# A cross-attention and expert layer on one core: row maxima turned in diagonal blocks, column-tile value products, the residual added in PSUM, routing in groups, a new step order

## What is computed

```python
B, S, D, H, FF, E, K = 16, 128, 128, 16, 512, 8, 2           # context rows SE = 77, HD = D // H = 8

def _attn(q_in, k_in, v_in, wq, bq, wk, bk, wv, bv, wo, bo, causal):
    Q, Kp, V = (heads of q_in @ wq + bq, k_in @ wk + bk, v_in @ wv + bv)
    scores = jnp.einsum('bqhd,bkhd->bhqk', Q, Kp) / jnp.sqrt(HD)      # causal: upper triangle -inf
    a = jax.nn.softmax(scores, axis=-1)
    return einsum('bhqk,bkhd->bqhd', a, V).reshape(B, S, D) @ wo + bo

def _moe(x, rw, rb, w1, b1, w2, b2):
    router_weights = jax.nn.softmax(x @ rw + rb, axis=-1)
    topw, topi = jax.lax.top_k(router_weights, K)
    topw = jax.nn.softmax(topw, axis=-1)
    combine = zeros((T, E)).at[rows, topi].add(topw)
    h = gelu(x @ w1[e] + b1[e]); eo = h @ w2[e] + b2[e]               # for every expert e
    return sum over e of eo * combine[:, e]

x = layernorm1(x + attn(x, x, x, sa weights, causal=True))
x = layernorm2(x + attn(x, context, context, ca weights, causal=False))
x = layernorm3(x + moe(x))
```

## Time and profile before

| | us |
|---|---|
| median of 3 runs | 497.91 (495.34 to 503.47) |
| the profiled execution: its own time | 495.67 |
| its span on the core | 493.6 |
| PE busy | 371.7 (75%) |
| DVE busy | 315.4 (64%) |
| ACT busy | 282.0 (57%) |
| POOL busy | 171.4 (35%) |

### The profile page before, as it was taken

How to read it: one execution, slowest core, us unless ns; L and a number is a source line. 1 busy time by engine, 2 the same in 40 slices (tenths; PEclk the granted TensorE clock), 3 DMA queues, 4 the chain that set the end, 5 groups by cost and what they waited for, 6 DMA issues and landing times.

```text
span 493.6 us, 8885 instructions
## 1 busy us (share of the span) xinstructions
PE 371.7 (75%) x2121; PEld 248.6 (50%) x2121; DVE 315.4 (64%) x1061; ACT 282.0 (57%) x648; POOL 171.4 (35%) x217
## 2 busy tenths in 40 slices
PE   2358779989988989999889997767603999999300
PEld 1323455565465465465465453353303999999300
DVE  9732555778778778778777877554371555555292
ACT  2017259679679679679679679516311555555132
POOL 9403112131441441431431432502120455554343
PEclk9999889999999999999999999965955999999855
DMA  8230302521341341350340340040872122221142
GB/s 223 82 74 0 71 16 49 140 51 29 84 131 30 82 134 28 82 141 19 88 131 24 88 138 12 24 137 18 259 184 52 42 70 64 60 62 51 55 124 85
DMA packets 38602, 39.92 MB, mean 81 GB/s; under 512 B 4762, under 2 KB 32271, under 8 KB 38552
## 3 DMA queue, kind: packets, MB, share of 16 engines
q1 hardware_dynamic: 36280, 35.11, 27.1%
q0 software_dynamic: 2272, 4.24, 2.5%
HBM read 13.66 MB, written 14.79 MB: 58 GB/s over the span
## 4 chain that ended last, share of the span: by engine, by line
PE 31%; DVE 25%; issue 11%; ACT 7%; DVEq 7%; DMA 7%; SPq 5%; POOL 3%; POOLq 0%; ACTq 0%
PE bank L535 6%; PE bank L479 4%; PE bank L522 4%; SPq L366 4%; DVEq L980 4%; PE bank L480 3%; DMA sa_km<-sa_ku 3%; ACT sa_qm L674 3%; PE bank L503 3%; DVE ca_nm L810 3%; DVE ca_us L983 2%; PE bank L502 2%; DVE yb L993 2%; PE bank L546 2%; ACT ca_qm L674 2%
## 5 line engine op out<-in xcount | busy, mean ns | idle before, releaser
L733 ACT ACTIVATE sa_us<-bank,expert_b 128x128 f32<-128x128 f32 x156 | 44.9, 367 | 48.8 <-PE bank L617 39.9
L1051 POOL TENSOR_SCALAR_AFFINE_SELECT sa_pt<-sa_pt 128x512 f32<-128x512 f32 x64 | 39.0, 635 | 71.5 <-ACT sa_pt L682 71.3
L1083 POOL DMA_INDIRECT results<-sa_us,xs x39 | 41.0, 1052 | 51.9 <-DVE sa_us L995 44.8
L810 DVE TENSOR_REDUCE sa_nm<-bank 128x4 f32<-128x512 f32 x64 | 41.6, 684 | 16.7 <-PE bank L503 16.5
L1074 POOL DMA_INDIRECT dispatched<-r_sent,r_row x32 | 31.8, 994 | 44.0 <-DVE r_sent L936 36.6
L617 PE MATMUL bank<-xsT,ca_us 128*128 128x128 f32 x312 | 45.2, 290 | 2.2 <-DVE ca_us L983 1.6
L674 ACT CAST sa_qm<-bank 8x512 fp32r<-8x512 f32 x64 | 36.9, 576 | 14.0 <-PE bank L510 12.4
L628 PE MATMUL bank<-ca_pt,sa_us 128*128 x312 | 43.8, 284 | 0.1
L674 ACT CAST ca_qm<-bank 8x512 fp32r<-8x512 f32 x64 | 36.8, 575 | 10.4 <-PE bank L510 9.2
L617 PEld LDWEIGHTS bank<-xsT,ca_us 128*128 128x128 f32 x312 | 39.4, 198 | 4.9 <-issue 3.1
L682 ACT ACTIVATE sa_pt<-bank 128x512 f32<-128x512 f32 x64 | 34.8, 597 | 10.4 <-PE bank L522 10.4
(11 more groups left out here) (210 smaller groups left out, 851.9 us busy)
## 6 DMA issues: line engine op xcount, KB each, us to landing
dispatched<-filler SPq DMA_DIRECT2D x17, 520.0 KB, 4.4
sa_km<-sa_ku SPq DMA_DIRECT2D x32, 96.0 KB
sa_qm<-sa_qu SPq DMA_DIRECT2D x32, 96.0 KB
ca_qm<-ca_qu SPq DMA_DIRECT2D x32, 96.0 KB
xs<-dispatched SPq DMA_DIRECT2D x39, 65.0 KB
sa_pt<-in_e_w SPq DMA_DIRECT2D x8, 256.0 KB, 5.2
ca_pt<-in_e_w SPq DMA_DIRECT2D x8, 256.0 KB, 6.1
sa_pt<-results SPq DMA_DIRECT2D x8, 256.0 KB, 4.7
```

The lines of the kernel that those rows point to most:

```text
L733: act.activation(hid[b][:, c, :], bank[2 * b + c // 2][:, P * (c % 2):P * (c % 2) + P], ACT.Gelu, bias=b1[:, bass.ds(expert * FC + c, 1)]) ...
L810: dve.tensor_reduce(k.nm[:, u, g, :], bank[home[k, "scores", u][g % 2]][:, :].rearrange("q (j n) -> q j n", j=J)[:, :, 0:k.keys], AX.X, AL ...
L1051: pool.affine_select(out=blockg, in_=blockg, compare_op=ALU.is_ge, fill=0.0, base=0, pattern=[[0, J], [1, P]], channel_multiplier=-1).then ...
L1083: pool.indirect_dma_start(out=results, out_offset=bass.IndirectOffsetOnAxis(ap=xs[v][:, P:P + 1].bitcast(I32), axis=0), in_=ys[v], in_offs ...
```

## The change

- `shift`: `mm` becomes [128, 2, 4, 4, 32], of which only the diagonal blocks are written; four transposes instead of one give `mT` with each head's maximum on its own 32 rows and columns, and ACT copies it once (128 x 512) in place of four casts. `weights` adds it by a second matmul for each group, with the selector `pick` (the rows `kones` broadcast) as stationary operand. The first matmul no longer waits for `shift`.
- `spread_terms`: the copies by SP take all 32 rows of each block (were 24), and DVE's operation is a plain copy.
- `mix`: 16 stationary operands of 32 columns for a sequence; each head goes to a column tile of its own, moving operand 128 columns, so one bank holds the whole sequence; one ACT copy and one `restore` of 4 transposes for a sequence where there were two.
- `norm`: one step for a pair. PE adds the residual into the bank by a matmul with the identity, for CA the bias by another; DVE no longer adds, and writes straight to `residual`, which `turn` and `route` read; POOL only takes the power, once for both.
- Routing in groups of pairs (0, 1), (2, 3, 4), (5, 6), (7): the logits of each pair are collected, and 27 DVE operations run once for the group on up to 6 tiles; the rank matmuls use totals of earlier groups; the indirect DMAs of a group (8, 12, 8, 4) go out together.
- `xs`, `ys`, `hid` and some table rows lie in tiles that the attention has done with. `ORDER` and `home` are new.

The core of the diff:

```diff
+def routed_together(pairs):
+    groups, left = [], list(range(pairs))
+    for size in (2, 3, 2):
+        if len(left) > size:
+            groups.append(tuple(left[:size]))
+            left = left[size:]
+    return groups + [(p,) for p in left]
...
         ORDER = [
+            (CA, 'restore', 1, -2), (CA, 'turn', 0, -1), (CA, 'mix', 2, -2), (CA, 'mix', 3, -2), (SA, 'shift', 0, 0),
+            (CA, 'project', 0, -1), (SA, 'values', 0, 0), (SA, 'turn', 0, 1), (CA, 'restore', 3, -2),
+            (CA, 'turn_heads', 0, -2), (CA, 'spread_terms', 0, -1), (RT, 'fill', 0, -2), (CA, 'spread_terms', 1, -1),
+            (CA, 'turn_heads', 1, -2), (CA, 'norm', 0, -2), (SA, 'weights', 0, 0), (SA, 'scores', 2, 0),
+            (RT, 'route', 0, -2), (RT, 'gate', 0, -2), (SA, 'scores', 3, 0), (SA, 'weights', 1, 0),
+            (SA, 'mix', 0, 0), (SA, 'shift', 1, 0), (RT, 'choose', 0, -2), (CA, 'scores', 0, -1),
+            (SA, 'weights', 2, 0), (RT, 'second', 0, -2), (CA, 'scores', 1, -1), (SA, 'mix', 1, 0),
+            (SA, 'weights', 3, 0), (RT, 'place', 0, -2), (CA, 'shift', 0, -1), (RT, 'number', 0, -2),
+            (CA, 'scores', 2, -1), (SA, 'project', 0, 1), (SA, 'restore', 1, 0), (SA, 'mix', 2, 0),
+            (SA, 'spread_terms', 0, 1), (SA, 'spread_terms', 1, 1), (SA, 'mix', 3, 0), (CA, 'weights', 0, -1),
+            (CA, 'scores', 3, -1), (CA, 'values', 0, -1), (SA, 'restore', 3, 0), (SA, 'turn_heads', 0, 0),
+            (CA, 'weights', 1, -1), (SA, 'turn_heads', 1, 0), (CA, 'shift', 1, -1), (CA, 'mix', 0, -1),
+            (CA, 'mix', 1, -1), (CA, 'weights', 2, -1), (SA, 'scores', 0, 1), (SA, 'norm', 0, 0),
+            (SA, 'scores', 1, 1), (CA, 'weights', 3, -1)]
...
                 for j in range(J):
-                    rows = slice(32 * j + 8, 32 * j + 32)
+                    rows = slice(32 * j, 32 * j + 32)
...
             def shift(k, p, u):                                      # TensorE
-                pe.transpose(bank[home[k, "shift", u][0]][:, 0:P], k.mm[:, u].rearrange("q j r -> q (j r)").bitcast(F32), ident).then_inc(k.s_mt_ps, 1)
+                for j in range(J):
+                    ins = pe.transpose(bank[home[k, "shift", u][0]][:, P * j:P * j + P], k.mm[:, u, j].rearrange("q i r -> q (i r)").bitcast(F32), ident)
...
             def weights(k, p, part):
-                pe.wait_ge(k.s_sha, p * 8 + 4 * u + 4)
...
+                    pe.matmul(bank[b][0:k.keys, :], k.ku[:, g, k.keys * u:k.keys * u + k.keys], k.qm[:, :, g, P * u:P * u + P], start=True, stop=False)
+                pe.wait_ge(k.s_sha, p * 2 + u + 1)
+                for g in pair:
+                    b = home[k, "weights", u][g % 2]
+                    pe.matmul(bank[b][0:k.keys, :], pick[:, g, 0:k.keys], k.mT[:, u].rearrange("r j n -> r (j n)"), start=False, stop=True).then_inc(k.s_s2_ps, 1)
...
             def mix(k, p, part):
-                    ins = pe.matmul(bank[b][64 * (g % 2):64 * (g % 2) + 64, :], k.vo[:, u, g, :], k.pt[u][:, 512 * g:512 * g + 512], start=True, stop=True)
+                    for j in range(J):
+                        ins = pe.matmul(bank[b][32 * j:32 * j + 32, P * g:P * g + P], k.vo[:, u, J * g + j, :],
+                                        k.pt[u][:, 512 * g + P * j:512 * g + P * j + P], start=True, stop=True)
...
             def norm(k, p, u):
+                pe.matmul(both, ident, residual[:, 2 * p:2 * p + 2, :], start=True, stop=False)
+                if not k.causal:
+                    pe.matmul(both, ident, k.bo.rearrange("q (o d) -> q o d", o=1).to_broadcast([P, 2, D]), start=False, stop=False)
+                for v in range(2):
+                    pe.wait_ge(k.s_ot, p * 2 + v + 1)
+                    ins = pe.matmul(both[:, v], k.oT[:, v, :], k.wo[:, :], start=False, stop=(v == 1))
...
             def shift(k, p, u):                                      # ScalarE
-                for j in range(J):
-                    rows = slice(32 * j, 32 * j + 8)
-                    src = bank[home[k, "shift", u][0]][rows, 0:P].rearrange("r (o n) -> r o n", o=1).to_broadcast([8, GROUPS, P])
-                    act.copy(k.qm[rows, j, :, P * u:P * u + P], src).then_inc(k.s_sha, 1)
+                act.copy(k.mT[:, u].rearrange("r j n -> r (j n)"), bank[home[k, "shift", u][0]][:, :]).then_inc(k.s_sha, 1)
...
             for k in KINDS:                                          # VectorE, setup
-                setup(dve.memset(k.vo[:, :, :, 32:64], 1.0))
-                setup(dve.memset(k.mm[:, :, :, :].bitcast(F32), 0.0))
+                setup(dve.memset(k.vo[:, :, :, HD:HD + 1], 1.0))
+                setup(dve.memset(k.vo[:, :, :, HD + 1:], 0.0))
+                setup(dve.memset(k.mm[:, :, :, :, :].bitcast(F32), 0.0))
...
+            setup(dve.tensor_copy(pick[:, :, :], kones.rearrange("r (g o) -> r g o", o=1).to_broadcast([P, GROUPS, P])))
...
             def number(k, p, u):                                     # GpSimd
+                n, group = group_of[p]
+                if p != group[-1]:
+                    return
                 pool.wait_ge(s_filled, p * 32 + 32)
...
-                for v in range(2):
+                for v in range(2 * len(group)):
                     for c in range(TOPK):
                         pool.indirect_dma_start(out=dispatched, out_offset=bass.IndirectOffsetOnAxis(ap=r.row[:, v, c:c + 1], axis=0),
```

More of the change, by code:

```diff
@@ L278, in build @@
-            (CA, "weights", 1, -1), (SA, "norm", 1, 0), (CA, "weights", 2, -1), (RT, "number", 0, -2),
-            (CA, "restore", 0, -1), (CA, "mix", 1, -1), (SA, "scores", 0, 1), (CA, "weights", 3, -1),
-            (CA, "restore", 1, -1), (CA, "mix", 2, -1), (SA, "scores", 1, 1), (CA, "turn_heads", 0, -1),
-            (CA, "turn", 0, 0), (RT, "fill", 0, -1), (CA, "mix", 3, -1), (SA, "shift", 0, 1), (CA, "norm", 0, -1),
-            (CA, "restore", 2, -1), (CA, "restore", 3, -1), (CA, "project", 0, 0)]
@@ L427, in _ @@
             held = {}
+            filling = set()
             def take(b):
+                assert b not in filling, b
                 for made, value in held.get(b, ()):
@@ L586, in place @@
+                for m in range(n):
+                    pe.matmul(dst, ones[:, :], r.total[:, m:m + 1, :].to_broadcast([P, tiles, EXPERTS]), start=False, stop=False)
+                for v in range(tiles - 1):
+                    for c in range(TOPK):
+                        last = v == tiles - 2 and c == TOPK - 1
+                        ins = pe.matmul(dst[:, v + 1:tiles, :], ones_bf[:, :], r.chosen[:, c, v:v + 1, :].to_broadcast([P, tiles - 1 - v, EXPERTS]), start=False, stop=last)
                 ins.then_inc(r.s_rank_ps, 1)
-                give(home[k, "place", u][0], r.s_rt, p * ROUTER_OPS + SELECTED + 6)
+                give(home[k, "place", u][0], r.s_rt, n * ROUTER_OPS + RANKED + 1)
```

403 lines of the change are left out of this document (210 added, 193 removed).

## The result

The change was measured at 508.09 us (median of 4 runs, 506.69 to 508.73) against 496.62 us for the kernel before (4 runs, 493.9 to 503.47): a ratio of 1.0246, 95% interval 1.0186 to 1.0305. The forecast was 478 us and faster. The profiled execution took 506.69 us with a span of 505.0 us.

The account below looks back on a forecast made before the run. PE was taken as the fullest engine in full iterations (33.1 of 36.8 us), latency as the matter in filling and emptying; -7 - 12 + 1 = -18 us on 495.67 gave 477.7, written 478, forecast between 470 and 488, wider range 460 to 498.

Parts of the forecast that it names:

- the sentence on POOL: Sends in groups of 8, 12, 8, 4: twelve hold POOL 15.5 us, so SA's `norm` power waits 2 to 3 us once.
- rival (2): The idle stays: PE waits elsewhere, for a bank or behind the new order; 495 to 497 us; chance 0.2.
- the full iterations: The five iterations between filling and emptying: 35.4 us each against 36.8, -7 us in all, bounds -12 to +6.5.
- load 34.4 and idle 1.0: PE in each full iteration: busy 34.4 us (+1.3), and 1.0 of the 3.7 us of idle taken to stay.
- the wait on `mm`: PE's wait on DVE's `mm`, 9.8 us in five full iterations, to fall under 1 us an iteration through lighter queues.
- m = 0.6: Time of one `mix` half on four column tiles, us, against 1.01 before; range 0.48 to 1.0, far end 1.8.
- rival (1): The `mix` column tiles are bound by issue, m = 1.0: 502 us, near 540 with m = 1.8; chance 0.12.
- ACT near 19 and DVE near 22.5 us: Busy time in each full iteration, down from 28.3 (ACT) and 28.9 us (DVE), far under PE.
- Setup +1: DVE's larger `mm` clearing, two strided parts of `vo` and `pick`, mostly hidden: +1 us, bounds 0 to +4.
- Filling and emptying -12: Shorter steps on the latency path before and after the full iterations, mainly `shift` casts and `mix`: -12 us, bounds -18 to -4.
- The copies at nothing: The 32-row copies move a third more bytes, 0 to 0.5 us of latency a copy; costed at nothing.
- `fill` at nothing: On SP, right ahead of CA's `spread_terms`, waiting for the previous group's sends, begun over 20 us earlier; costed at nothing.

Follow-up runs that it names:

- sitting 4: One of seven sets of kernels measured one after another on one chip; changed kernel, unedited, against the kernel before: 484.62 us against 493.17, ratio 0.983, semaphores 0.1 us late at most.
- sittings 1, 2 and 6: The three sets with late semaphores; changed kernel, unedited, 508.09 and 509.57 us in first and last; in the middle one, sends cut otherwise, 507.02 us.
- sitting 1: The set of the result on record: changed kernel, unedited, 508.09 us against 496.62 for the kernel before, ratio 1.025, semaphores up to 12.3 us late.
- the kernel before with sends against memsets: Kernel before with four more sends a pair into an unread tensor (eight in a row), 540.79 us; with ten memsets a pair in their place, 539.61 us.
- sitting 2: Set with the kernel before at 493.48 us; changed kernel with sends cut otherwise 507.02 us, ratio 1.029, semaphores up to 8.0 us late.
- groups of one: Changed kernel with every pair routed by itself, four sends in a row eight times: 507.33 us, ratio 1.028; in a later set 501.52 us median, none late.
- two rows of four a pause apart: Changed kernel with groups of two pairs, sends split into fours, three later routing steps moved: 477.22 us without late semaphores, 508.26 us (1.027) with them.

## Why the prediction was wrong

**What failed in the number on record** is the sentence on POOL: that sends in rows of 8, 12 and 8 hold POOL, and that its power waits "2 to 3 us once". As a price of the held engine this was right: in sitting 4 the power stands right behind the twelfth send and PE waits 2.6 us for the residual, once.

```profile
274.91 0.96 POOL L1127 DMA_INDIRECT dispatched<-r_sent,r_row  x1 [0.30 <-issue]
275.89 0.74 POOL L1116 TENSOR_TENSOR sa_rs<-sa_ba,half 128x2 f32<-128x2 f32 x1
...
277.33 0.44 PE L465 MATMUL bank<-cst,residual 128*128 128x128 f32 x2 [2.58 <-DVE residual L907]
```

But in sittings 1, 2 and 6 TensorE's semaphores also come late in the rows of sends, 24.5 us of standstill in sitting 1, and the sum has nothing for it. No row of before shows that; its trace has it only as semaphores up to 1.05 us late at the fourth send, which cost nothing there. No rival named it; rival (2) has the words "the sends hold POOL", not this mechanism nor this size. Shown: what stands still, when, and that its size is that of the difference between two measurements of one kernel (24.5 against 23.5 us), though not to the microsecond: behind the standstills PE's granted clock is at 0.50 for longer (274.8 to 288.5 us, in sitting 4 277.7 to 284.5), and they cover the 2.6 us wait shown above. Not shown: what makes one sitting different. It is not the program, which was the same; not the chip alone; and not the moment at which the row falls. Whether the recording of events has a part in it is open. That the sends are needed rests on their coinciding in every trace and on the kernel before with sends against memsets in sitting 2.

**What failed besides**, where nothing is stalled: the full iterations. 35.4 us each were forecast, 177 for five; they take 183.3, so -0.5 instead of -7. Of the two terms, load 34.4 and idle 1.0, the load was 0.8 too high (PE is busy 167.8 us in the five, 33.6 each) and the idle far too low (15.5 us in the five, 3.1 each). Without routing it is 32.5 busy and 1.9 idle in 34.4 us, and the sum is near by two errors that nearly cancel. It fails in the two iterations of the five that carry a group's arithmetic (39.9 and 38.4, of them 4.9 and 4.7 idle). The forecast averaged DVE's load over all iterations (14.5 operations a pair), but a group's 27 operations come in one iteration, ahead of the cross-attention's maxima, and PE waits for these. Windows of sitting 4 around that wait:

```profile
145.00:150.00 5.00, 2.38 (x29) 1.41 (x29) 4.55 (x17) 1.94 (x5) 2.19 (x4) 1.00 0.00 2
150.00:155.00 5.00, 4.98 (x36) 3.96 (x36) 3.18 (x11) 1.53 (x3) 2.50 (x3) 0.66 0.07 23
```

DVE is 91% busy, PE 48%; then PE's granted clock is 0.66 in the mean, part of it at the lower level, and the same `mix` half starts 1.01 us ahead of its successor instead of 0.58. I named the wait on `mm` as what the lighter queues would shorten; they did, save here.

**Point by point for the rest.** The `mix` half: 152.50 - 151.92 = 0.58 us for the m = 0.6 taken, so rival (1) was wrong and the row of bf16 pairs a good guide. The Trainium skill's page "TensorE: Matmul & The Clock Gate", section "Wait — 56ns, not 53.3ns?", gives about 62 ns for each matmul with hardware decode off. The 16 instructions in 0.58 us are 36 ns each, so that bound doesn't hold here, and no run tells how decode was set. ACT near 19 and DVE near 22.5 us: over the five iterations 20.0 and 23.6. Setup +1: +0.4 (first `ku` 21.7 against 21.3 us). Filling and emptying -12: -6.9 - 3.8 = -10.7 in sitting 4. The copies at nothing: 0.5 us apart. `fill` at nothing: SyncE waited 15.9 us at the longest for the sends in sitting 4, and PE waited no more than 0.2 us for a `km` copy in the full iterations. The expert part, 91.7 us, as before. Without stalls the sum is 0.4 - 6.9 - 0.5 - 3.8 = -10.8 and the span differs by 493.6 - 483.2 = 10.4: 484.6 and 482.4 us, inside the range and 4 to 7 us above the 478 written.

## What to carry to other kernels

A load that is batched must be costed in the iteration in which it lands, at its place in the queue, not as a mean; what it delays is the next thing behind it that another engine needs. And a change of 2% that moves where many indirect DMAs fall has to be measured in more than one sitting, with the kernel before beside it: four runs that agreed within 0.4% said 508, and nine of ten others in two other sittings said 478 to 486 (the tenth, unexplained, 916). Where a time moves so between sittings, look at the semaphore events too: how late they are against the instructions that make them, and how many the trace holds.

## What the runs showed of the hardware

In three sittings of seven, TensorE's semaphores came up to 12.3 us after the recorded end of their matmuls while GpSimd issued indirect DMAs, 1.26 us apart; in the other four, under the same sends, they were 0.01 to 0.05 us late, with single ones of the column-tile matmuls up to 0.32. The semaphores of the other engines were within 0.07 us in all. The latest was 1.05 us with the rows of four of before, 2.4 with groups of one, 4.5 with two rows of four a pause apart and with the eight of before, 8.1 with the changed kernel's eight and 12.3 with its twelve. In the kernel before with eight sends the late ones arrived in steps, one for each send (139.4, 140.8, 142.2 us with sends at 138.7, 140.0, 141.3); in the changed kernel all that had piled up arrived within 0.2 us, 1.8 us after the last send's end in the group of eight and 2.6 us in that of twelve. In the sittings with late semaphores the trace of the same program also held 13 to 17% fewer semaphore updates (three programs were traced in both kinds of sitting).

In sitting 4, after a wait of PE of 2.4 us its granted clock fell to the lower level, from 151.4 to 154.9 us (0.66 in the mean from 150 to 155 us). After waits of 1.1 us in other iterations it stayed at 1.00, and so it did after a wait of 2.05 us at 259.1 us.
